# Sharing out the elementwise work of the projection stage among three engines

## The reference, cut to what matters

```
# out: attention output, per token 16 heads of 16 values
rms = rsqrt(mean(out * out, axis=-1) + EPS)      # per token and head
out = out * rms * gamma
out = (1.0 - LAMBDA_INIT) * out
attn = out.reshape(B, T, C) @ w_proj
x = x + attn + ffn(xn)                           # residual, first layer
xn = _layernorm(x)                               # (x - mean) / sqrt(var + eps), per token
```

## Time and profile before

| | us |
|---|---|
| median of 3 runs | 3957.22 (3954.38 to 3958.09) |
| the profiled execution | 3959.01 |
| its span in the trace | 3957.2 |
| projection stage, first PE instruction to last DMA issue | 2534.5 to 2612.1 |

### The profile page before, as it was taken

The page is one execution under the profiler, slowest core; times in us unless marked ns, Lnnn a source line. Parts: engine busy times, 40 slices in busy tenths (PEclk is TensorE's granted clock), DMA queues, the critical chain, the costliest instruction groups (busy, mean ns, idle before and its releaser), DMA issues. The chain is left out here.

```text
span 3957.2 us, 58039 instructions
## 1 busy us (share of the span) xinstructions
PE 3582.2 (91%) x18836; PEld 1535.7 (39%) x18837; DVE 2921.1 (74%) x4699; ACT 2240.7 (57%) x3500; POOL 1478.3 (37%) x1789
## 2 busy tenths in 40 slices
PE   5997999979999999999999999647999999999998
PEld 3554666513333333333333333332344344343344
DVE  3553222268888888888888887357899999898998
ACT  2331222217777777777777777416667666666663
POOL 1220000022332333323322323205677676776765
PEclk9998999959999999999999999878999999999999
DMA  6332111110100011111101100230000000000000
GB/s 207 105 102 63 45 45 45 41 31 28 30 27 25 29 31 31 31 31 31 31 28 31 30 25 21 66 116 6 11 6 17 6 11 12 6 17 11 6 11 6
DMA packets 119993, 143.58 MB, mean 36 GB/s; under 512 B 24184, under 2 KB 100224, under 8 KB 119728
## 3 DMA queue, kind: packets, MB, share of 16 engines
q1 hardware_dynamic: 101760, 105.12, 8.8%
q0 software_dynamic: 6144, 16.79, 1.3%
q10 hardware_dynamic: 11824, 18.35, 1.3%
HBM read 86.98 MB, written 52.43 MB: 35 GB/s over the span
## 5 line engine op out<-in xcount | busy, mean ns | idle before, releaser
L1170 DVE TENSOR_REDUCE pmax<-psR 128x1 f32<-128x512 f32 (+3 forms) x2240 | 1370.0, 669 | 264.1 <-PE psR L1220 174.8
L1111 ACT ACTIVATE prob<-psS 128x1024 f32<-128x1024 f32 (+3 forms) x1280 | 1103.0, 904 | 402.5 <-PE psS L1268 395.8
L1893 POOL TENSOR_TENSOR hc<-h_d,crep 128x512 f32<-128x512 f32 x512 | 667.0, 1307 | 367.4 <-DVE h_d L2149 214.6
L1220 PE MATMUL psR<-kslab,qslab 48*128 48x512 bf16 (+3 forms) x2560 | 729.4, 359 | 66.9 <-DMA kslab<-k_d 29.7
L1268 PE MATMUL psS<-qslab,kslab 51*128 51x512 bf16 (+3 forms) x2560 | 646.6, 351 | 4.9 <-ACT prob L1111 4.4
L1283 PE MATMUL psVo<-prob,vaug 128*32 128x512 f32 (+3 forms) x5120 | 625.1, 544 | 0.9 <-ACT ov L1115 0.9
L1043 POOL TENSOR_SCALAR_AFFINE_SELECT prob<-prob 128x256 f32<-128x256 f32 (+1 forms) x512 | 209.8, 422 | 867.9 <-ACT prob L1111 867.6
L2357 PE MATMUL psYd<-hc,ident 128*128 128x512 f32 x1024 | 523.8, 600 | 0.3 <-POOL hc L1893 0.2
L2149 DVE TENSOR_TENSOR_SCAN h_d<-a,state,psU 128x512 f32<-128x512 f32 x384 | 489.0, 1274 | 0.3
L1220 PEld LDWEIGHTS psR<-kslab,qslab 48*128 48x128 bf16 x2560 | 191.4, 94 | 762.2 <-DVE pmax L1170 414.0
L2139 DVE TENSOR_TENSOR psU<-dtx,psX 128x512 f32<-128x512 f32 x512 | 353.8, 691 | 56.0 <-POOL dtx L1881 12.5
(11 more groups left out here) (273 smaller groups left out, 4812.5 us busy)
## 6 DMA issues: line engine op xcount, KB each, us to landing
x_e<-rows_d SPq DMA_DIRECT2D x72, 128.0 KB, 2.0
y_d<-y SPq DMA_DIRECT2D x72, 128.0 KB, 1.7
q_d<-parts SPq DMA_DIRECT2D x48, 128.0 KB, 2.3
k_d<-parts SPq DMA_DIRECT2D x48, 128.0 KB, 2.6
qslab<-q_d SPq DMA_DIRECT2D x64, 96.0 KB
kslab<-k_d SPq DMA_DIRECT2D x64, 96.0 KB
wg<-n_L_ffn_gate_proj_w_dram ACTq DMA_DIRECT2D x8, 512.0 KB, 10.6
x<-in_L_attn_x_dram SPq DMA_DIRECT2D x8, 512.0 KB, 5.3
```

Source lines behind the costliest of these rows:

```text
L1111: act.activation(prob[g % BUFS][:, :, off:BLK], psS[g % 2][:, :, off:BLK], ACT.Exp).then_inc(prob_ready, 1)
L1170: dve.tensor_reduce(pmax[:, a].rearrange("p i c -> p (i c)")[:, lo:lo + (count - 1) * NEXT + 1:NEXT], psR[at % BANKS][:, 0:count * w].rear ...
L1220: ins = pe.matmul(dst[:, m * w:(m + 1) * w], qslab[u][rows, i * P:(i + 1) * P], kslab[u][rows, ch * BLK:ch * BLK + w], start=(m == 0), sto ...
L1893: pool.tensor_tensor(hc[:, g % CR], h[:, g % HR], crep[:, g // PAIR % SPR], ALU.mult).then_inc(hc_ready, 1)
```

## The change

The squares move from GpSimd to ACT (`square_heads`, an activation with Square). The scaling of the heads (y_c) and of the tokens (xn_c) moves from DVE to GpSimd (`scale_heads`, `scale_tokens`), with the same four instructions for each. DVE keeps the sums, the reciprocals, the residual and the statistics. The reciprocal of n waits for y_c of n - 1, as before. In the state space phase two semaphores that nothing uses are no longer made.

```diff
         @block.gpsimd
         def _(pool):
+            def scale_heads(n):
+                pool.wait_ge(inv_ready, n + 1 + CREDIT)
+                pool.wait_ge(yT_done, n + CREDIT)
+                ob = heads_of(n)
+                for j in range(TPB):
+                    ins = pool.tensor_tensor(y[:, j].rearrange("p (h d) -> p h d", h=HEADS), ob[:, :, j],
+                                             inv[:, :, j:j + 1].to_broadcast([P, HEADS, VD]), ALU.mult)
+                ins.then_inc(y_ready, 1)
+
+            def scale_tokens(n):
+                pool.wait_ge(rstd_ready, n + 1 + CREDIT)
+                pool.wait_ge(xT_done, n + CREDIT)
+                for j in range(TPB):
+                    ins = pool.tensor_scalar(xn[:, j, :], x1[n % 2][:, j, :], mv[:, j, 0:1], rstd[:, j:j + 1],
+                                             ALU.subtract, ALU.mult)
+                ins.then_inc(xn_ready, 1)
+
+            for n in range(AHEAD):
+                scale_heads(n)
             for n in range(NBLK):
-                pool.wait_ge(ss_ready, n + CREDIT)
-                ob = heads_of(n)
-                pool.tensor_tensor(sq[:], ob, ob, ALU.mult).then_inc(sq_ready, 1)
+                scale_tokens(n)
+                if n + AHEAD < NBLK:
+                    scale_heads(n + AHEAD)

         @block.scalar
         def _(act):
+            def square_heads(n):
+                act.wait_ge(ss_ready, n + CREDIT)
+                act.activation(sq[:], heads_of(n), ACT.Square).then_inc(sq_ready, 1)
+
...
+            square_heads(0)
             for n in range(AHEAD):
                 head_root(n)
+                square_heads(n + 1)
                 copy_heads(n)
             for n in range(NBLK):
                 token_root(n)
                 if n + AHEAD < NBLK:
                     head_root(n + AHEAD)
+                if n + AHEAD + 1 < NBLK:
+                    square_heads(n + AHEAD + 1)
                 copy_out(n)
...
             def head_norm(n):
                 dve.wait_ge(root_ready, n + 1 + CREDIT)
-                if n:
-                    dve.wait_ge(y_ready, n + CREDIT)
+                dve.wait_ge(y_ready, n + CREDIT)
                 dve.reciprocal(inv[:], root[:]).then_inc(inv_ready, 1)
-                dve.wait_ge(inv_ready, n + 1 + CREDIT)
-                dve.wait_ge(yT_done, n + CREDIT)
-                ob = heads_of(n)
-                for j in range(TPB):
-                    ins = dve.tensor_tensor(y[:, j].rearrange("p (h d) -> p h d", h=HEADS), ob[:, :, j],
-                                            inv[:, :, j:j + 1].to_broadcast([P, HEADS, VD]), ALU.mult)
-                ins.then_inc(y_ready, 1)
...
             def token_norm(n):
                 dve.wait_ge(std_ready, n + 1 + CREDIT)
                 dve.reciprocal(rstd[:], std[:]).then_inc(rstd_ready, 1)
-                dve.wait_ge(rstd_ready, n + 1 + CREDIT)
-                dve.wait_ge(xT_done, n + CREDIT)
-                for j in range(TPB):
-                    ins = dve.tensor_scalar(xn[:, j, :], x1[n % 2][:, j, :], mv[:, j, 0:1], rstd[:, j:j + 1],
-                                            ALU.subtract, ALU.mult)
-                ins.then_inc(xn_ready, 1)
```

More of the change, by code:

```diff
@@ L1647, in phase_state_space @@
         halo_ready = sem("d_halo_ready")
-        sz_copied = sem("d_sz_copied")
         sz_ready = sem("d_sz_ready")
@@ L1666, in phase_state_space @@
         y_added = sem("d_y_added")
-        state_zero = sem("d_state_zero")
         high_ready = sem("d_high_ready")
```

## The result

The changed kernel takes 3973.08 us (median of 6 runs, 3970.65 to 3973.91), the kernel before 3957.07 us in the same comparison. The ratio is 1.0041, 95% interval 1.0028 to 1.0054: slower by 0.4%. The prediction was 3952.3 us, in a range up to 3962.5; it is wrong in sign and in size.

What follows compares the result with a forecast made beforehand. VectorE was taken as the stage's bound. Start +0.3, middle -6.0 and end +0.8 us summed to -4.9 us, so 3957.2 became 3952.3 us, in a range of 3948 to 3962.5.

Steps and rivals of the forecast that it cites:

- The bound: Middle of the stage: VectorE, busy 39.10 of 40 us, sets the 9.34 us block and stops being the bound after the change.
- Squares on ACT, cost 0: ACT's added square per block, about 1.07 us, is hidden under 4.5 us of cover and costs 0.
- Heads on GpSimd, H = 2.4: H, the four GpSimd multiplications scaling a block's heads, takes 2.4 us, or 2.9 by the row without broadcast.
- Tokens on GpSimd, T between 1.6 and 2.9: T, the four GpSimd instructions scaling a block's tokens, takes 1.6 to 2.9 us; 2.2 was taken.
- The chain T + H + 2.8: Block period: token scaling, head scaling, then 2.8 us of transposes, copy, root and reciprocal; 7.4 us.
- The other limit, 7.26 us: PE with ACT, through transposes, copies and projection: no block can take less than 7.26 us.
- Six places for each us of T: Each extra us of token scaling counts once in four periods, once at the start and once at the end.
- The rival "scaling of tokens is dear": GpSimd's two-factor token scaling costs more than assumed: +7.9 us at 1.08 us an instruction; chance 0.22, of which 0.11 slower.
- The clock: PE's granted clock, 1.00 in mid-stage; the sum had no term for a fall.
- The small `vare` beside GpSimd, cost 0: VectorE's small `vare` may wait 2.4 us for a group of heads, yet costs 0 in the middle.

Runs made afterwards that it cites:

- squares_only: Changed kernel with both scalings back on DVE, so only the squares move to ACT: 3954.25 us, ratio 0.9984 to the kernel before.
- half_project: Changed kernel with half of each PE projection left out (result wrong): 3972.00 us, one execution.
- tokens_imm: Changed kernel with two constants in place of the mean and the reciprocal in the scaling of tokens: 3972.37 us, one execution.
- root_ahead: Changed kernel with the root of the next block's tokens ahead of the copy of yT in ACT's order: 3975.59 us, ratio 1.0037 to the kernel before.
- tokens_copy: Changed kernel with a plain GpSimd copy in place of the scaling of tokens: 3956.02 us, ratio 0.9992 to the kernel before.
- tokens_oneop: Changed kernel with the subtraction of the mean left out of the scaling of tokens, one operation remaining: 3965.88 us, one execution.
- tokens_gp: Changed kernel with the scaling of heads back on DVE, tokens still on GpSimd: 3969.79 us, ratio 1.0024 to the kernel before.
- squares_eps: squares_only without DVE's small var and vare, ACT's root taking scale and EPS itself: 3950.73 us, ratio 0.9985 to the kernel before.

## Why the prediction was wrong, point by point

- **The bound.** VectorE bound the stage before, and no longer does: 39.10 to 21.25 of 40 us. Right.
- **Squares on ACT, cost 0.** Right: 1.05 us each, and squares_only has the period that VectorE's work without the stall gives.
- **Heads on GpSimd, H = 2.4.** Right: 2.46.
- **Tokens on GpSimd, T between 1.6 and 2.9.** This is the step that failed; it measured 4.84. The bounds were rows of other forms, a copy and a product of two tensors, and the trace had no row of this one. That every GpSimd row of the size lay between 0.40 and 0.74 us was no evidence for a form that was not among them. An upper end taken from the dearest neighbour is no bound.
- **The chain T + H + 2.8.** Right: 9.94 us against 10.1; the changed kernel's rows follow it link by link, and half_project shows that the projection is not in it. The prediction did not name the second loop, over two blocks and through the projection; it rules in tokens_imm, where projections run at the lower clock, and in root_ahead.
- **The other limit, 7.26 us.** Right: 7.33 to 7.36 in tokens_copy.
- **Six places for each us of T.** Nearly: with T = 4.84 it gives +10.9 us of the 14.0, and a seventh place (the period after the start, 8.84 us before, so set by the chain above T of about 3.6) makes it 11.7 with H and the period as measured. tokens_oneop agrees with seven places, tokens_imm does not, as its clock fell.
- **The rival "scaling of tokens is dear".** It is what happened. It was priced well: slower beyond 1.08 us an instruction, and 1.22 was measured. Its chance, 0.11 for slower, rested on rows of other forms; nothing in the trace spoke for this form's price either way.
- **The clock.** I took it as no worse than before. It costs 1.5 us of the 14 here, and 2.6 of the 7.5 us in squares_only.
- **The small `vare` beside GpSimd, cost 0.** It waits as supposed: it ends with the heads in this row, 1.93 instead of 0.17 us, and the chain did not need it by then.

```profile
2552.29 2.44 POOL L1401 TENSOR_TENSOR y_c<-o_all,inv 128x256 f32<-128x256 f32 x4
...
2552.83 1.93 DVE L1498 TENSOR_SCALAR vare<-mv_c 128x4 f32<-128x4 f32 x1
```

Elsewhere it slips in between two of GpSimd's instructions. In half_project it takes 0.72 us and ends at 2550.84, while the heads go on until 2552.01:

```profile
2549.57 2.44 POOL L1401 TENSOR_TENSOR y_c<-o_all,inv 128x256 f32<-128x256 f32 x4
...
2550.12 0.72 DVE L1498 TENSOR_SCALAR vare<-mv_c 128x4 f32<-128x4 f32 x1
```

Two rules of the Trainium skill were weighed. What the Trainium skill says in "SBUF — State Buffer", section "Who interferes with whom", of the shared port pair is borne out: xn_c at 1.38 us in squares_only, `vare` at 1.93 here, and GpSimd's xn_c at 5.30 beside y_c in tokens_gp, so either side may be the one that waits. The section speaks of a lock for one instruction; at 2552.83 `vare` waited until the last of GpSimd's four heads had ended, and in half_project only until the second had. The Trainium skill, in "GPSIMD Engine Reference", section "Engine selection", calls GpSimd about twice as slow for two inputs and roughly at line rate for one. The runs come near it for two (2.46 against 1.43 us, 1.7 times) and not for the scaling: 4.84 against 1.39 us, 3.5 times. For GpSimd's copy (0.40 us) no VectorE row of the same form stands beside it.

## What to carry to other kernels

Price an instruction on a new engine by a row of its own form; where the trace has none, the upper end has to stay open, or the form is run once by itself before anything is moved. When work leaves the bounding engine, write down the loop that closes behind it through the other engines' orders, with each link's row: here it was right to 0.2 us, and it also says that every us of the moved instruction counts once a block, as long as no other loop is longer. Cutting such a loop by an edit of the order ties another one; follow the new one before running it.

## What the runs showed of the hardware that I had not expected

- A GpSimd operation with a factor (128x256, f32) takes 0.92 us with one operation and one per-partition factor, 1.07 with two operations and two constants, 1.22 with two operations and two per-partition factors, against 0.40 for a copy and 0.65 for a product of two tensors with a broadcast.
- Back-to-back GpSimd instructions can shut out a VectorE instruction of 128x4 for the rest of the group, up to 1.93 us instead of 0.17; in half_project (2550.12) it got through in the middle of a group, after 0.72.
- The granted clock fell in two projections, one behind the other, in the middle of the stage in squares_only and squares_eps (5.0 instead of 3.32 us), and was back at the upper level for the transposes between them (1.04 us); the kernel before kept 1.00 from 2560 to 2600. A shorter period of the other engines is partly given back there.
